# A decoder layer on one core: geometric product and q and k transposes moved to the head of the next turn, projection moved up, low parts made by GpSimd

## What is computed

```python
# 1. attention, 8 heads of 32, 2 heads of k and v, causal, block by block
out = softmax(causal(q @ k.T * DH**-0.5)) @ v
qp, kp = q[..., :3] @ dirs, k[..., :3] @ dirs          # a direction per head
geo_out = softmax(causal(qp[:, None] * kp[None, :])) @ v
x = x + (out + head_scale * (geo_out - out)) @ Wo
# 2. weighted history: for each channel a decaying sum over time, k = layernorm(x), v = context
y_t = (sum_e*v up to t-1, decayed, + exp(first + k_t) * v_t) / (the same without v)
x = x + y
# 3. feed-forward: Hadamard transform, 8 bit rounding, ternary weights, silu(gate) * up, the same again, down
x = x + ffn(layernorm(x))
```

## Time and profile before

| | |
|---|---|
| median of 3 runs | 450.31 us (449.54 to 451.16) |
| the profiled execution | 450.48 us, span from first to last instruction 448.7 us |
| busy in the span | PE 368.2 us (82%), DVE 355.1 (79%), ACT 269.5 (60%), POOL 110.0 (25%) |
| mean granted clock of TensorE | 0.953 of full speed |
| attention turns | about 14.7 us each, r = 3 to 15 with all five stages |

### The profile page before, as it was taken

How to read it: one execution, slowest core, us unless ns; L and a number is a source line. 1 busy time by engine, 2 the same in 40 slices (tenths; PEclk the granted TensorE clock), 3 DMA queues, 4 the chain that set the end, 5 groups by cost and what they waited for, 6 DMA issues and landing times. The chain is left out here.

```text
span 448.7 us, 7687 instructions
## 1 busy us (share of the span) xinstructions
PE 368.2 (82%) x2354; PEld 253.9 (57%) x2354; DVE 355.1 (79%) x936; ACT 269.5 (60%) x534; POOL 110.0 (25%) x160
## 2 busy tenths in 40 slices
PE   2988878898788878887888876597888999989794
PEld 1754554555455545454545444375767777777573
DVE  4586878988899889888986567888979889897642
ACT  1254566566766676657675555668748585675542
POOL 1210312220222022202230123432333333232210
PEclk9988999999999999999998588798999999999899
DMA  7960012000000000000000000000000000000001
GB/s 217 292 203 0 2 31 88 12 1 15 12 13 1 13 12 14 2 11 15 12 6 7 13 1 0 1 2 0 1 24 11 15 14 12 25 2 23 12 25 36
DMA packets 13711, 13.43 MB, mean 30 GB/s; under 512 B 2007, under 2 KB 12887, under 8 KB 13543
## 3 DMA queue, kind: packets, MB, share of 16 engines
q1 hardware_dynamic: 13671, 12.94, 9.8%
HBM read 10.84 MB, written 2.10 MB: 29 GB/s over the span
## 5 line engine op out<-in xcount | busy, mean ns | idle before, releaser
L695 PE MATMUL wide<-had,c_h_hi 128*128 128x512 f32 x128 | 55.8, 436 | 8.6 <-ACT c_q2T L475 8.1
L412 POOL TENSOR_TENSOR c_h_lo<-c_hb,c_h_hi 128x512 fp32r<-128x512 f32 x32 | 40.8, 1273 | 74.6 <-ACT c_h_hi L464 69.3
L695 PE MATMUL wide<-had,c_h_lo 128*128 128x512 f32 x128 | 53.2, 415 | 0.0
L680 PE MATMUL wide<-c_q_T,w_tern_all 128*128 128x256 bf16 x256 | 36.5, 283 | 7.6 <-DVE c_hh L1029 6.0
L457 ACT ACTIVATE c_sl<-c_z 128x512 f32<-128x512 f32 x32 | 20.1, 629 | 31.6 <-DVE c_z L1020 31.4
L906 PE MATMUL bank<-w_o,a_att 128*128 128x256 f32 x128 | 32.9, 401 | 2.9 <-DVE a_att L1191 2.2
L695 PEld LDWEIGHTS wide<-had,c_h_hi 128*128 128x128 f32 x128 | 25.5, 199 | 15.8 <-issue 10.8
L680 PEld LDWEIGHTS wide<-c_q_T,w_tern_all 128*128 128x128 bf16 x256 | 23.6, 101 | 18.3 <-DVE c_hh L1029 8.1
L378 POOL TENSOR_TENSOR a_qk<-a_rot_c,a_rot_s 128x320 f32<-128x320 f32 x16 | 13.8, 865 | 71.7 <-DVE a_rot_s L1162 71.7
L1029 DVE TENSOR_TENSOR c_hh<-wide,c_sl 128x512 f32<-128x512 f32 x32 | 22.1, 691 | 10.2 <-ACT c_sl L457 10.2
L906 PEld LDWEIGHTS bank<-w_o,a_att 128*128 128x128 f32 x128 | 23.9, 196 | 11.0 <-DVE a_att L1191 7.2
(11 more groups left out here) (188 smaller groups left out, 1007.6 us busy)
## 6 DMA issues: line engine op xcount, KB each, us to landing
x_res<-in_x SPq DMA_DIRECT2D x4, 512.0 KB, 7.5
b_vT<-in_ctxT SPq DMA_DIRECT2D x16, 128.0 KB, 2.2
out<-c_yo SPq DMA_DIRECT2D x16, 128.0 KB, 1.7
w_raw_all<-in_wg SPq DMA_DIRECT2D x1, 1024.0 KB, 8.7
w_raw_all<-in_wu SPq DMA_DIRECT2D x1, 1024.0 KB, 10.8
w_raw_all<-in_wd SPq DMA_DIRECT2D x1, 1024.0 KB, 13.2
had_f<-in_h SPq DMA_DIRECT2D x1, 1024.0 KB, 4.8
w_o_raw<-in_Wo SPq DMA_DIRECT2D x4, 128.0 KB, 6.7
```

Of the source, the lines that this page charges most:

```text
L412: nc.gpsimd.tensor_tensor(h_lo[p][:, j::FQ, :], hb[j % 2][:, :].rearrange("c (m t) -> c m t", m=2), h_hi[p][:, j::FQ, :].bitcast(F32), ALU ...
L680: mm = nc.tensor.matmul(dst[:, m * TOK:(m + 1) * TOK], w[:, k * FF + blk * P:k * FF + blk * P + P], q_T[p][:, k * TOK:(k + 1) * TOK], star ...
L695: mm = nc.tensor.matmul(wide[:, 1 + i, m * 512:(m + 1) * 512], a[p][:, j + FQ * m, i * P:(i + 1) * P], had512[:, j, :], start=(j == 0 and ...
```

## The change

No arithmetic changes; the same instructions stand in another order, and two move to another engine:

- PE: the turn begins with the q and k transposes of m (before: at the end of the previous turn), then the transposes of x of f, then the geometric product of b (before: in the turn of m; for the last block it stays there). Scores of m; projection of f; row transposes of m; products with v of b; transposed scores of m, key transposes of c, product of the row maxima (which waits for the transposed scores through a new semaphore `sT`), output projection of b, transposes of y of d. The eight extra matmuls without use in turn 1 are gone.
- ACT: `qkT` of m first, `xT`, `e_g` of b, the ternary piece (before: last), the row copies, `v_in`, `decays`, then the pair of d, the pair of b, high parts of q and k, `e_s`, high parts of the directions.
- DVE: scans of d first, normed keys, row maxima, sums of d, rotation, running maximum and small row operations, attended values, y of d, diagonal of m, directions, layer norm, residual sum of d, then of b, statistics.
- POOL: after `qk` the two low parts, which wait for both high parts, and then the products with the context.

The diff, cut (moved pieces stand where they arrive):

```diff
 # POOL body, behind qk
+                        need(pool, A["hi"], 2 * (u + 1))
+                        need(pool, A["tq"], u - 1)
+                        qv = split_q[p][:, :].rearrange("t (h s d) -> t h s d", h=H, s=2)
+                        nc.gpsimd.tensor_tensor(
+                            qv[:, :, 1, :], qk[p][:, 0:H * DH].rearrange("t (h d) -> t h d", h=H),
+                            qv[:, :, 0, :].bitcast(F32), ALU.subtract).then_inc(A["lo"], 1)
+                        kv = split_k[p][:, :].rearrange("t (s g r d) -> t s g r d", s=2, g=KVH, r=4)
+                        nc.gpsimd.tensor_tensor(
+                            kv[:, 1], spread(qk[p][:, H * DH:QKW].rearrange("t (g d) -> t g d", g=KVH), 2, 4),
+                            kv[:, 0].bitcast(F32), ALU.subtract).then_inc(A["lo"], 1)
...
 # ACT body
+                def geometric_weights(u, p):
+                    need(act, A["geo"], u + 1)
+                    need(act, A["pn"], u - 1)
+                    nc.scalar.activation(e_g[p][:, :], geo[:, :], ACT.Exp).then_inc(A["eg"], 1)
...
                 def body(f, m, b, c, d):
+                    if m is not None:
+                        u, p = m
+                        need(act, A["tq"], u + 1)
+                        need(act, A["nm"], u - 1)
+                        nc.scalar.copy(qkT[p][:, :], scores[:, :]).then_inc(A["qT"], 1)
                     if f is not None:
...
                         nc.scalar.copy(xT[p][:, :], turn[:, 0:C]).then_inc(A["xT"], 1)
+                    if b is not None and b[0] < NB - 1:
+                        geometric_weights(*b)
+                    if m is not None and m[0] >= 4:
+                        ternary(m[0] - 4)
...
                     if c is not None and m is not None:
                         decays(*c)
+                    if d is not None:
+                        u, p = d
+                        need(act, B["dnm"], u + 1)
...
                     if b is not None:
                         u, p = b
                         need(act, A["pd"], u + 1)
...
+                    if f is not None:
+                        u, p = f
+                        need(act, A["qk"], u + 1)
...
                     if m is not None:
                         u, p = m
                         need(act, A["nm"], u + 1)
                         need(act, A["pn"], u - 1)
                         nc.scalar.activation(e_s[p][:, :], scoresT[:, :], ACT.Exp, scale=SCALE).then_inc(A["es"], 1)
...
 # PE body
+                def geometric(u, p):
+                    need(pe, A["eg"], u)
+                    need(pe, B["en"], KC * (u - 1))
+                    for g in range(2):
+                        nc.tensor.matmul(geo[:, g * 512:g * 512 + 512], ident_b[:, :], mask_st[:, :],
+                                         start=True, stop=True)
+                    need(pe, A["stk"], u + 1)
+                    need(pe, A["gd"], u + 1)
...
                 def body(f, m, b, c, d):
+                    if m is not None and m[0] == NB - 1:
+                        turn_x(0, 0)
+                    if m is not None:
+                        u, p = m
+                        need(pe, A["hi"], 2 * (u + 1))
+                        need(pe, A["lo"], 2 * (u + 1))
+                        need(pe, A["mx"], u)
+                        need(pe, A["stk"], u)
+                        for j, sp in enumerate([split_q[p]] * 4 + [split_k[p]] * 4):
...
+                        mm.then_inc(A["tq"], 1)
+                    if f is not None:
...
+                        mm.then_inc(A["t1"], 1)
+                    if b is not None and b[0] < NB - 1:
+                        geometric(*b)
...
                         mm.then_inc(A["s"], 1)
+                    if f is not None:
...
                         mm.then_inc(A["proj"], 1)
...
                         mm.then_inc(A["rows"], 1)
...
                             mm.then_inc(A["pd" if den else "pn"], 1)
+                    if m is not None:
+                        u, p = m
+                        need(pe, A["es"], u)
...
+                        mm.then_inc(A["sT"], 1)
+                    if c is not None and m is not None:
+                        keys(*c)
...
                     if m is not None:
+                        u, p = m
+                        need(pe, A["sT"], u + 1)
+                        need(pe, A["mrow"], 2 * (u + 1))
...
                         mm.then_inc(A["nm"], 1)
+                    if m is not None and m[0] == NB - 1:
+                        geometric(*m)
```

More of the change, by code:

```diff
@@ L564, in body @@
                         nc.scalar.activation(e_s[p][:, :], scoresT[:, :], ACT.Exp, scale=SCALE).then_inc(A["es"], 1)
[L565 to L587, removed]
-                        nc.scalar.activation(invb[p][:, :], lnb[p][:, :], ACT.Exp, scale=-1.0).then_inc(B["inv"], 1)
+                    if m is not None and m[0] == NB - 1:
+                        geometric_weights(*m)
                     if f is not None:
                         u, p = f
-                        need(act, A["tq"], u + 1)
-                        need(act, A["nm"], u - 1)
-                        nc.scalar.copy(qkT[p][:, :], scores[:, :]).then_inc(A["qT"], 1)
                         need(act, A["dir"], u + 1)
@@ L611, in body @@
                                                  accum_out=w_abs[:, n:n + 1]).then_inc(s_wabs, 1)
-                    if m is not None and m[0] >= 4:
-                        ternary(m[0] - 4)
                 def feed(f, m, h, b):
@@ L849, in body @@
                             idle_work(scoresT, 16)
-                    if c is not None and m is not None:
-                        keys(*c)
                     if m is not None:
                         u, p = m
-                        need(pe, A["mrow"], 2 * (u + 1))
-                        for h in range(H):
-                            mm = nc.tensor.matmul(scoresT[:, h * P:h * P + P], pick_neg[:, h * P:h * P + P],
-                                                  m_row[p][:, :], start=False, stop=True,
-                                                  skip_group_check=True)
-                        mm.then_inc(A["nm"], 1)
+                        need(pe, A["mx"], u + 1)
+                        nc.tensor.transpose(rows[0:8, 0:P], mx[p][:, :], ident[:, :])
+                        need(pe, A["dir"], u + 1)
+                        for a in range(2):
+                            nc.tensor.transpose(rows[0:40, (1 + a) * P:(2 + a) * P], proj_d[p][:, 64 * a:64 * a + 40], ident[:, :])
+                        need(pe, A["hl"], 4 * (u + 1))
+                        for a in range(2):
+                            mm = nc.tensor.transpose(rows[0:64, (3 + a) * P:(4 + a) * P].bitcast(F32R),
+                                                     dir_hl[p][:, 64 * a:64 * a + 64], ident_r[:, :])
+                        mm.then_inc(A["rows"], 1)
                     if b is not None:
@@ L884, in body @@
                         u, p = m
[L885 to L896 removed]
+                        need(pe, A["sT"], u + 1)
+                        need(pe, A["mrow"], 2 * (u + 1))
+                        for h in range(H):
+                            mm = nc.tensor.matmul(scoresT[:, h * P:h * P + P], pick_neg[:, h * P:h * P + P],
+                                                  m_row[p][:, :], start=False, stop=True,
                                                   skip_group_check=True)
[L898 removed]
+                        mm.then_inc(A["nm"], 1)
+                    if m is not None and m[0] == NB - 1:
+                        geometric(*m)
                     if b is not None:
@@ L1268, in body @@
                     if d is not None and d[0] < NB - 2:
-                        context_now(*d)
+                        context_add(*d)
                     if b is not None:
@@ L1288, in body @@
                                                     decay_e[:, k:k + 1], None, ALU.mult).then_inc(s_grd, 1)
-                    if d is not None and d[0] < NB - 2:
-                        context_add(*d)
                     if b is not None:
```

186 lines of the change are left out of this document (78 added, 108 removed).

## The result

The changed kernel takes **515.6 us** (median of 4 runs, 512.74 to 518.33); the kernel before takes 449.93 in the same comparison. Ratio 1.1456, with a 95% interval of 1.1387 to 1.1525. The profiled execution took 512.74 us, with a span of 511.0 against 448.7 and a mean granted clock of 0.895 against 0.953.

A forecast was written before the change was run, and what follows sets the result against it. A ring of waits through the engines was taken to bound the turn: 17.3 us, 19.5 with the clock's fall, 4.7 more than now. 450.5 + 61 for 13 turns + 1.5 - 2.5 gave 511 us, range 476 to 551.

The forecast's parts named there:

- The ring: Chain of waits through the engines, from the row transposes to the next ones: turn 17.3 us, 2.5 more.
- The clock: Granted clock falls at PE's stall before the output projection in nearly every turn: 2.2 us more, turn 19.5.
- rival 3: Stall before the product with v brings a second clock fall: 22.2 us a turn, 547 us; chance 0.24.
- The low parts on POOL: Two subtractions moved to POOL take 1.4 us, in time with 0.5 us of cover; nothing charged.
- Rival 2: Clock holds, low parts come 1.0 us too late by DVE and POOL's SBUF port rule: 496 us; chance 0.10.
- The ends: Turns 1 and 2 save 2.5 us (0 to 5), turn 16 costs 1.5; feed-forward part unchanged.
- Rival 4: Keys and exponentials don't stand behind the product with v, turn 12.9 us or so: 426 us; chance 0.05.

The follow-up runs named there:

- the clock's mend: The changed kernel with 11 matmuls without use in PE's stall ahead of the output projection, turns 3 to 15: 523.02 us, 1.1633 of the kernel before.
- the port's: The changed kernel with only the two low parts back on DVE, behind the attended values: 507.36 us, 1.1285 of the kernel before.

## Why the prediction was right, and where it wasn't

It said 511 us, with 476 to 551, and slower with 0.93. The median is 515.6. The ring, the main mechanism, was right; that the total came so near is in part luck, since errors cancel in two places, as said below. By its steps:

- **The ring of waits: right, in place and size.** 17.3 us a turn were added up; 17.01 were measured in steady turns where clock and port were both out of the way. One move of the key transposes makes the kernel before as slow as the changed one; moving them back takes 57 us off the changed one, moving ACT's exponentials behind b's pair 70 (some of that by freeing DVE's tail). The three waits are the predicted ones: 2.87 us before the output projection (3.1 expected), 1.53 before the product with v (1.61; the profile names `v_now` there, the copy that ends 0.1 us before v_in), 3.85 before the key exponentials at 195.15 (3 to 4). The geometric product waits no more in the steady turns. Nothing in the busy shares of the earlier trace rows pointed to it.
- **The clock: the fall came, its price was another.** It falls behind the predicted stall, for 3.4 or 6.8 us, some 5.2 a turn (5 were taken); the second fall of rival 3, over the product with v, came in one turn of the 13 (171.6 to 174.9). But the 2.2 us a turn weren't there to be won: with full clock over the output projection the turn stayed at 18.5, and with the port out of the way as well the clock gave back 1.0 on average. The step that failed is the one that added 2.2 to the ring as if nothing else ran beside the output projection.
- **The low parts on POOL: charged nothing, which was wrong.** The prediction looked only at whether the low parts themselves would be in time; they were. Their price is on DVE: y 0.42 to 0.99 us, diagonal 1.22 to 1.74, directions' first product 0.20 to 0.68, POOL's own product with the context 0.69 to 1.66, and the transposes of x, which the change had put at the head of the turn, wait for the end of that tail. Rival 2's rule (Trainium skill, SBUF — State Buffer, "Who interferes with whom": a DVE instruction with two SBUF inputs and a GpSimd one that reads SBUF shut each other out) agrees with this trace: the diagonal took 0.52 us more with 0.65 of the low part left. Rival 2's size, 1.0 us a turn, was near: with the clock up, 18.51 against 17.01 is 1.5. Its path was wrong, and so was the expectation that DVE's busy time would drop by 2 us: it rose by 0.4.
- **Both together.** Against the mean turn of 19.11, the clock's mend gave 19.84, the port's 18.79, both 17.78. The mean turn of 19.1 is the ring's 17.0, 1.5 for the two covers (18.50 in steady turns) and 0.6 for turns longer than that, by long falls of the clock and by what makes turns 8, 12 and 15 long in other kernels, too. The prediction had 17.3 and 2.2. The sum per turn came out nearly right (19.5) with the clock's term too large and the port's missing; that they nearly cancel is luck.
- **The ends.** From turn 16 on: 1.5 expected, 1.5 measured, which tests little, as this part took 202 to 211 us in the traces of the other kernels. Turns 1 and 2: 2.5 us of gain expected, 4.4 of loss measured. The step took "no keys, so a shorter ring" and left out that the transposes of x, moved ahead of geometric product and scores, make these wait for a layer norm that comes late in the first turns. That order is what the trace shows (4.80 us, 32.58); that it is the whole cause was not shown: with it moved back, no kernel got faster beyond its scatter.
- In the sum: 13 turns gave 56.4 for 61 (4.6 too much), the ends 5.9 for -1 (6.9 too little), and so the profiled execution lies 2 us over the forecast, again by errors that cancel. The median is another 3 us above that execution.

Rival 4's figure, 426 us where the ring doesn't close, was not reached: with the ring open the turn is 14.54 or 13.98, and 13.28 with the low parts on DVE as well, where 12.9 was taken. DVE is busy for 12.71 us of such a turn and PE for 11.91, so little is left to win by order alone; that was not tried.

## What to carry to other kernels

When a piece is moved in an in-order list, follow the dependencies once round through all engines' lists and add up durations along that ring; busy shares don't show it. When the sum has two delays side by side, ask for each what would be late next if it were gone: here the clock's half speed and the DVE tail stretched by POOL covered each other. Removing one made the kernel 7 us slower or 8 faster, removing both made it 19 faster. Work taken off DVE and given to POOL can make DVE busier, 13.32 us a turn against 12.02 here. Whether it does depends on what it falls beside: with the same low parts on POOL behind the diagonal DVE was busy for 11.44.

## What the runs showed of the hardware that wasn't expected

- Two engines blocking each other lose on both sides: POOL's product of 128x256 took 0.69 us with the low parts on DVE and 1.66 beside DVE's diagonal, which went from 1.22 to 1.74. DVE's busy time per turn, 13.32, was 1.3 us above that of the kernel with the low parts on DVE (12.02), which has more DVE instructions (33 against 31).
- Keeping PE busy ahead of the output projection kept the clock up there, but moved the fall: it came behind the next wait, of 1.70 us, and over work with no cover (0.57 in the window 227 to 231 of that run). Filling one stall made the kernel 7 us slower.
- An added float32 product of 128 columns cost 0.235 us (22 in 5.18), so filling a stall of 2.9 us takes about twelve and not 22.
- The low stretches of the clock in the changed kernel's turns are 3.4 or 6.8 us long. The short ones cost nothing beside DVE's stretched tail (18.50 against 18.51 with the clock up), the long ones 0.3 to 0.5 us in steady turns.
